# Cross-attention projections turn over three PSUM banks in a decoder layer on one NeuronCore

## The reference

```python
x = _layernorm(x + _L0_attn_ref(x, ...), axis=-1)          # causal self-attention, one head of 256
x = _layernorm(x + _L0_xattn_ref(x, ctx_2048, mask, ...), axis=-1)
x = _layernorm(x + _L0_ffn_ref(x, ...), axis=-1)           # 64 experts, 8 per token, one shared expert
...
    q = (hidden_states @ Wq + bq).reshape(b, s, NH, HD)    # 16 heads of 128
    k = (encoder_hidden_states @ Wk + bk)                  # 4 key/value heads of 128
    v = (encoder_hidden_states @ Wv + bv)
    q = _rmsnorm(q, qn_w)
    k = _rmsnorm(k, kn_w)
    scores = jnp.einsum('bhsd,bhed->bhse', q, k) * scale
    ...
    return out.transpose(0, 2, 1, 3).reshape(b, s, NH * HD) @ Wo
```

## Time and profile before

| | |
|---|---|
| median of 3 runs | 1892.0 us (1889.64 to 1893.38) |
| the profiled execution | 1891.63 us, its span 1889.9 us |
| TensorE matmul busy | 1547.4 us, 82% of the span |
| TensorE weight loads | 1255.8 us, 66% |
| VectorE busy | 1265.1 us, 67% |
| ScalarE busy | 688.6 us, 36% |
| GpSimd busy | 1050.4 us, 56% |

### The profile page before, as it was taken

The page is one execution under the profiler, slowest core; times in us unless marked ns, Lnnn a source line. Parts: engine busy times, 40 slices in busy tenths (PEclk is TensorE's granted clock), DMA queues, the critical chain, the costliest instruction groups (busy, mean ns, idle before and its releaser), DMA issues. The chain is left out here.

```text
span 1889.9 us, 34753 instructions
## 1 busy us (share of the span) xinstructions
PE 1547.4 (82%) x9744; PEld 1255.8 (66%) x9744; DVE 1265.1 (67%) x3827; ACT 688.6 (36%) x1526; POOL 1050.4 (56%) x1023
## 2 busy tenths in 40 slices
PE   4799998999899898989999864777777878787685
PEld 3687877778788787777878753555555656555453
DVE  3688877877778887888888844345555555433486
ACT  3344444343443343434344411222232222222353
POOL 3457666666566666666666742445555545555321
PEclk7799999999999999999999976889999898988799
DMA  7323231222212111121111295655565655554496
GB/s 244 118 91 104 73 106 62 94 82 89 89 62 95 63 59 67 45 75 47 66 59 52 81 277 157 182 165 160 162 182 161 181 160 172 172 167 129 169 417 278
DMA packets 182979, 246.41 MB, mean 130 GB/s; under 512 B 30972, under 2 KB 159561, under 8 KB 178388
## 3 DMA queue, kind: packets, MB, share of 16 engines
q1 hardware_dynamic: 149188, 169.71, 28.7%
q0 software_dynamic: 27648, 69.28, 10.0%
q10 hardware_dynamic: 6032, 6.13, 0.9%
HBM read 136.19 MB, written 117.19 MB: 134 GB/s over the span
## 5 line engine op out<-in xcount | busy, mean ns | idle before, releaser
L1555 POOL DMA_INDIRECT expert_out_scratch<-y,target x320 | 318.7, 996 | 296.6 <-DVE y L1779 196.0
L558 POOL DMA_INDIRECT slot_scratch<-xrow x256 | 258.7, 1010 | 188.6 <-DVE xrow L1174 117.1
L598 PE MATMUL bank_c<-wq_w,x1t 128*128 128x512 f32 x768 | 215.4, 433 | 62.9 <-DVE q_work L1016 53.7
L598 PEld LDWEIGHTS bank_c<-wq_w,x1t 128*128 128x128 f32 x768 | 154.6, 209 | 113.1 <-DVE q_work L1016 67.8
L1614 PE MATMUL bank_g<-gu,x_turned 128*128 (+1 forms) x1408 | 217.1, 303 | 14.9 <-issue 12.4
L503 POOL TENSOR_TENSOR q_rs<-q_ve,minus_half 128x8 f32<-128x8 f32 x64 | 137.4, 2147 | 146.6 <-DVE q_ve L1005 142.9
L1614 PEld LDWEIGHTS bank_g<-gu,x_turned 128*128 128x128 f32 x1408 | 194.4, 214 | 31.0 <-issue 30.5
L1633 PE MATMUL bank_y<-dp,inter_t 64*128 (+1 forms) x352 | 137.2, 473 | 85.2 <-DVE y L1779 60.0
L1671 ACT ACTIVATE x_turned<-bank_x 128x512 f32<-128x512 f32 x176 | 105.3, 598 | 272.8 <-PE bank_x L1596 161.1
L1770 DVE TENSOR_TENSOR inter<-silu,bank_g 128x128 f32<-128x128 f32 x176 | 50.2, 285 | 220.1 <-ACT silu L1678 144.7
L744 PE MATMUL bank_d<-wo_w,o2t 128*128 128x256 f32 x1536 | 194.5, 287 | 2.0 <-DVE o2t L933 2.0
(11 more groups left out here) (240 smaller groups left out, 3305.3 us busy)
## 6 DMA issues: line engine op xcount, KB each, us to landing
x_rows<-slot_scratch SPq DMA_DIRECT2D x320, 136.0 KB
results<-expert_out_scratch SPq DMA_DIRECT2D x32, 1024.0 KB, 10.1
slot_scratch<-zeros SPq DMA_DIRECT2D x16, 816.0 KB, 4.2
dp<-in_down SPq DMA_DIRECT2D x161, 64.0 KB
slot_scratch<-zeros SPq DMA_DIRECT2D x8, 1088.0 KB, 9.4
gu<-in_gate_up SPq DMA_DIRECT2D x11, 768.0 KB
expert_out_scratch<-y,target POOLq DMA_INDIRECT x320
token_row_scratch<-xrow SPq DMA_DIRECT2D x32, 136.0 KB
```

Of the source, the lines that this page charges most:

```text
L558: nc.gpsimd.indirect_dma_start(out=slot_d[:, :], out_offset=bass.IndirectOffsetOnAxis(ap=xrow[slot][:, SLOT8 + k:SLOT8 + k + 1].bitcast(U3 ...
L598: last = nc.tensor.matmul(target, left[a][:, c, :], right(b, c), start=(n == 0 and c == 0), stop=(n == len(PASSES) - 1 and c == C - 1))
L1555: nc.gpsimd.indirect_dma_start(out=y_d[:, :], out_offset=bass.IndirectOffsetOnAxis(ap=target[n % 8][:, j:j + 1], axis=0), in_=y[s % 4][:, ...
```

## The change

- Three banks take turns for the projections: `turns` is bank_c's two and bank_e. Query groups 0 to 3 use banks 0, 1, 2, 0 of it, keys bank 1, values bank 2 (bank_e).
- Query group 2 no longer waits for a bias. It waits until bank_e is free: turned keys of the previous tile copied, and the routing count of three tiles back done. Group 3 waits for bias 0, keys for bias 1 and values for bias 2.
- Since keys and values no longer pass behind biases 2 and 3 in bank_c, the query transposes wait for the fourth bias (`q_biased` 4t + 4) and `k_biased`; the wait for `v2_copied` moves to the routing transpose, which uses bank_e after the values.
- `bank_r` is another name for bank_e where the routing uses it. No instruction is added or taken away but for a few sequencer rows.

```diff
+        bank_r = bank_e[:, 0, 0:D]
+        turns = [bank_c[:, 0, :], bank_c[:, 1, :], bank_e[:, 0, :]]
...
                 if g < 2:
                     pe.wait_ge(sig["cross_masked"], 2 * t)
+                elif g == 2:
+                    pe.wait_ge(sig["kt_copied"], t)
+                    if not (isinstance(t, int) and t < 3):
+                        pe.wait_ge(sig["counted"], t - 2)
                 else:
-                    pe.wait_ge(sig["q_biased"], 4 * t + g - 1)
-                product(bank_c[:, g % 2, :], x1t, lambda b, c: wq_w[b][:, c, g * 512:(g + 1) * 512])\
+                    pe.wait_ge(sig["q_biased"], 4 * t + 1)
+                product(turns[g % 3], x1t, lambda b, c: wq_w[b][:, c, g * 512:(g + 1) * 512])\
                     .then_inc(sig["q_projected"], 1)
...
+                pe.wait_ge(sig["q_biased"], 4 * t + 2)
+                product(turns[1], ctxt, lambda b, c: wkv_w[b][:, c, 0:KW]).then_inc(sig["k_projected"], 1)
+
+            def value_project(t):
                 pe.wait_ge(sig["q_biased"], 4 * t + 3)
-                product(bank_c[:, 0, :], ctxt, lambda b, c: wkv_w[b][:, c, 0:KW]).then_inc(sig["k_projected"], 1)
-
-            def value_project(t):
-                pe.wait_ge(sig["q_biased"], 4 * t + 4)
-                product(bank_c[:, 1, :], ctxt, lambda b, c: wkv_w[b][:, c, KW:2 * KW]).then_inc(sig["v2_projected"], 1)
+                product(turns[2], ctxt, lambda b, c: wkv_w[b][:, c, KW:2 * KW]).then_inc(sig["v2_projected"], 1)
...
                 if n:
                     pe.wait_ge(sig["qt_copied"], 2 * t + 1)
                 else:
+                    pe.wait_ge(sig["q_biased"], 4 * t + 4)
                     pe.wait_ge(sig["k_biased"], t + 1)
-                    pe.wait_ge(sig["v2_copied"], t + 1)
...
                 pe.wait_ge(sig["x2_normed"], t + 1)
                 pe.wait_ge(sig["counted"], t)
-                transpose_in(bank_e[:, 0, :], xrow[slot]).then_inc(sig["x2_transposed"], 1)
+                pe.wait_ge(sig["v2_copied"], min(t + 3, TILES) if isinstance(t, int) else t + 3)
+                transpose_in(bank_r, xrow[slot]).then_inc(sig["x2_transposed"], 1)
```

More of the change, by code:

```diff
@@ L696, in key_transpose @@
                 pe.wait_ge(sig["k_normed"], t + 1)
-                if not (isinstance(t, int) and t < 2):
+                if isinstance(t, int) and t < 2:
+                    pe.wait_ge(sig["v2_copied"], t + 1)
+                else:
                     pe.wait_ge(sig["logits_copied"], t - 1)
@@ L758, in route_score @@
                 for c in range(C):
-                    last = nc.tensor.matmul(bank_e[:, 0, 0:EXPERTS + 1], x2t[:, c, :], router_w[:, c, :],
+                    last = nc.tensor.matmul(bank_r[:, 0:EXPERTS + 1], x2t[:, c, :], router_w[:, c, :],
                                             start=(c == 0), stop=(c == C - 1))
@@ L767, in rank @@
                 pe.wait_ge(sig["kt_copied"], min(t + 3, TILES) if isinstance(t, int) else t + 3)
-                nc.tensor.matmul(bank_e[:, 0, 0:EXPERTS], before[:, :], chosen[:, :], start=True, stop=True)
-                nc.tensor.matmul(bank_e[:, 0, EXPERTS:2 * EXPERTS], ones[:, :], chosen[:, :], start=True, stop=True)\
+                nc.tensor.matmul(bank_r[:, 0:EXPERTS], before[:, :], chosen[:, :], start=True, stop=True)
+                nc.tensor.matmul(bank_r[:, EXPERTS:2 * EXPERTS], ones[:, :], chosen[:, :], start=True, stop=True)\
                     .then_inc(sig["ranked"], 1)
@@ L848, in copy_values @@
                 act.wait_ge(sig["v2_biased"], t)
-                copy("v2_copied", v2_new[:, :], bank_c[:, 1, :], "v2_projected", t + 1)
+                copy("v2_copied", v2_new[:, :], turns[2], "v2_projected", t + 1)
                 if isinstance(t, int) and t == 0:
@@ L857, in copy_x2 @@
                 act.wait_ge(sig["routed"], t)
-                copy("x2t_copied", flat(x2t[:, :, :]), bank_e[:, 0, 0:D], "x2_transposed", t + 1)
+                copy("x2t_copied", flat(x2t[:, :, :]), bank_r, "x2_transposed", t + 1)
             def copy_keys(t):
@@ L998, in bias_keys @@
                 dve.wait_ge(sig["k_projected"], t + 1)
-                nc.vector.tensor_tensor(flat(k2[:, :, :]), bank_c[:, 0, :], bkv_b[:, 0:KW], ALU.add)\
+                nc.vector.tensor_tensor(flat(k2[:, :, :]), turns[1], bkv_b[:, 0:KW], ALU.add)\
                     .then_inc(sig["k_biased"], 1)
@@ L1015, in query_bias @@
                 dve.wait_ge(sig["q_projected"], 4 * t + g + 1)
-                nc.vector.tensor_tensor(q_work[:, g * 512:(g + 1) * 512], bank_c[:, g % 2, :],
+                nc.vector.tensor_tensor(q_work[:, g * 512:(g + 1) * 512], turns[g % 3],
                                         bq_b[:, g * 512:(g + 1) * 512], ALU.add).then_inc(sig["q_biased"], 1)
@@ L1087, in route_choose @@
                 dve.wait_ge(sig["routed"], n1)
-                nc.vector.tensor_copy(logits[:, :], bank_e[:, 0, 0:EXPERTS + 1]).then_inc(sig["logits_copied"], 1)
+                nc.vector.tensor_copy(logits[:, :], bank_r[:, 0:EXPERTS + 1]).then_inc(sig["logits_copied"], 1)
                 wait_alone(dve, sig["logits_copied"], n1, sig["dve_held"])
@@ L1157, in place @@
                 dve.wait_ge(sig["ranked"], n1)
-                nc.vector.tensor_tensor(ranks[:, :], bank_e[:, 0, 0:EXPERTS], count[:, :], ALU.add)\
+                nc.vector.tensor_tensor(ranks[:, :], bank_r[:, 0:EXPERTS], count[:, :], ALU.add)\
                     .then_inc(sig["placed"], 1)
-                nc.vector.tensor_tensor(count[:, :], bank_e[:, 0, EXPERTS:2 * EXPERTS], count[:, :], ALU.add)\
+                nc.vector.tensor_tensor(count[:, :], bank_r[:, EXPERTS:2 * EXPERTS], count[:, :], ALU.add)\
                     .then_inc(sig["counted"], 1)
```

## The result

The changed kernel takes 1868.1 us (median of four runs, 1857.9 to 1876.0) against 1891.3 us (four runs) for the kernel before on the same chip: ratio 0.987 (95% interval 0.983 to 0.992), some 23 us or 1.3% faster. The profiled execution took 1860.3 us, its span 1858.6; it is one of the two faster ones of the four (the others took 1875.9 and 1876.0).

A forecast was written before the change was run, and what follows sets the result against it. An attention step was taken to be as long as TensorE's free run plus VectorE's chain after the scatter burst. 1891.6 - 18.9 + 5 = 1877.7, taken as 1878 us, 0.75% faster; range 1858 to 1895, the forecast's own 1868 to 1887.

The forecast's parts named there:

- Group 2 in the third bank: Attention loop: query group 2 starts without waiting for a bias, removing VectorE's idle before biases 2 and 3: -18.9 us.
- Late-bias steps: Attention steps where biases 0 and 1 wait, 2 and 3 do not; low clock moves to transposes, keys, values: +5 us.
- rival (b): Attention loop: early-bias steps turn into the late-bias kind, which takes longer: 1908 us; chance 0.04.
- early-bias steps: Attention steps where the residual addition starts late and biases 2 and 3 wait for their groups; 1.86 us idle goes.
- Keys and values: Keys in the second bank and values in the third, each one bias earlier: no separate gain, 0.
- New waits: Routing transpose waiting for the values' copy, and extra sequencer rows: bounded by 0 and 3 us, taken as 0.
- Rival (a): Low clock falls on transposes, keys and values in every attention step, 1.2 us each: up to 1906 us; chance 0.26.
- Rival (c): The scatter burst costs less and more attention steps become like the 31.4 us one: about 1852 us; chance 0.12.
- Rival (d): Query group 2 still starts after bias 0 because the routing count comes late: 1892 us; chance within 0.16.
- What would show it: Trace signs: three query groups unbroken, idle before biases 54.7 to about 36 us, transposes' wait 21.7 to 35 or more.
- The reading of remote: VectorE's remote waits are TensorE completions coming late during GpSimd's scatter burst, visible about 1.1 us after the sixth scatter.

The follow-up runs named there:

- the filler's run: Kernel before with eight extra matmuls, results unread, into the third bank ahead of query group 2: 1884.7 us, ratio 0.998.
- group 2 only: Changed kernel with only query group 2 in the third bank, values back in a bank of bank_c: 1870.2 us, 0.988 of the kernel before.
- the two kernels of chip 10: The changed kernel unaltered once more, 1864.8 us, ratio 0.988, and group 2 only, 1870.2 us, 0.988, beside the kernel before at 1889.9 us.
- values only: Kernel before with only the values moved to the third bank, queries and keys as they were: 1887.8 us, ratio 0.998.
- the moved scatters: Changed kernel with scatters before and after GpSimd's power split none and eight, three and five, or four and four: 2042.9, 1873.3, 1834.2 us.
- four and four: Four scatters before GpSimd's power and four after, instead of six and two: changed kernel 1834.2 us, 0.952; kernel before 1836.2 us, 0.953.
- the moved burst: Changed kernel with all eight scatters sent after GpSimd's power for the residual addition's norm: 2042.9 us (one run).
- the last run: Changed kernel with scatters four and four and the key squares on ScalarE instead of GpSimd: 1612.4 us, 0.986 of the kernel before (1634.6 us).

## Why the prediction was right, and where it was wrong

The time came out inside the range and inside the forecast's own range, faster, as forecast, by 1.3% instead of 0.75%. The mechanism of the gain was right. One of the two terms had its net sign wrong, and part of the loop's gain lies in idle that the sum did not touch, so the nearness of 1878 and 1868 is in part luck. The measurement also tells less than the forecast took: its interval is 0.983 to 0.992, and not 0.2% wide to each side.

- *Group 2 in the third bank, -18.9 us.* Right: the idle before biases 2 and 3 went from 18.9 to 1.0 us, and TensorE's wait before the transposes grew by 18.8 us: VectorE's chain stayed the later one. That the two numbers agree is chance; on chip 10 this wait came to 36.3 and 33.9 us with the same gain. What the step did not ask is where those 18.9 us came from; some 8 of them were groups at the low clock (the filler's run). The sum needed no split, since the bank removes both.
- *Late-bias steps, +5 us.* This term was too large, and what the clock did as a whole went the other way. I moved the low clock from groups 2 and 3 to the transposes, keys and values, since a pause of over 2 us seemed to stay. (Six steps with a wait before bias 0 had held a low stretch before, and not four.) That does happen, but seldom and cheaply. At 826.12 a pause of 2.21 us was followed by transposes and keys at the low clock (1.97 and 2.41 us; 1.09 and 1.63 at full pace). TensorE's wait before the query transposes took up most of it (0.35 us, and 1.45 in a like step), and the step took 33.9 us instead of 33.5: 0.4 us, not 1.2. It was one step of this profile; in the second profile of the changed kernel five steps took 3.7 to 4.6 us for keys and values. In most others the pause was shorter: at 432.94 it was 1.57 us and six keys behind it took 1.64, full pace. The low level within the loop fell from 44.4 us to 10.2 (20.5 and 17.1 in the two other profiles of the changed kernel, 17.1 with group 2 only). TensorE now works through group 2 in the time it had waited, so its longest wait before a query group is 1.4 us and not 2.8. Taken at nothing, the sum would have been 1891.6 - 18.9 = 1872.7, nearer to 1868.
- *What the sum left out, -5.7 us.* The idle before the residual addition and biases 0 and 1 fell from 66.4 to 60.7. It was 61.3 and 61.1 in the two kernels of chip 10 with the same gain, but 59.1 in values only, whose time stayed, and 73.4 in the changed kernel on chip 2 against 71.4 on chip 1 before. So it varies from execution to execution and chip to chip, and I can't put it down to the change. In some steps the kind did change: rival (b) had early-bias steps become late-bias and cost; here three steps whose biases 0 and 1 had waited got a longer wait before the residual addition and none before bias 1 instead, as at 492.49 (1.07 us), and took 31.8 us against 34.2. Why is open.
- *Keys and values, 0.* Right: values only is 0.998 (0.995 to 1.001), and group 2 only has the whole gain. *New waits, 0.* Right: idle put down to issue before the query groups is 1.8 us after and was 6.1, and the values' copy hides behind the query scaling.
- *Rival (a), the low clock in every step*, did not come: pauses of 1.3 to 1.6 us went with a granted clock of 1.00 and 0.99. The warning of the Trainium skill, "TensorE: Matmul & The Clock Gate", section "A second HAM failure mode: psum-queue depth-cycling", that turning over banks with short pauses makes the clock fall back again and again, doesn't hold for this kernel; the measurement decides. *Rival (c)*, cheaper steps, came in a small way: its 1852 was not reached by any median. Its yardstick was misread, too. The step of 31.4 us was not an early-bias step without low clock as such, but one whose residual addition had waited 1.8 us; those that wait 3.2 us took 32.3 after the change, with no low clock in them. *Rival (d)* is excluded by the order of the rows.
- *What would show it.* Groups 0 to 2 without pause, no idle before biases 2 and 3, transposes' wait over 35 us, and keys and values no longer than before (2.98 to 3.03 us together before; 2.99 to 3.02 after in 27 of 28 steps, 3.78 in the one of 826.12): seen but for that step. The idle before biases came to 25.8 and not 36 in this profile, to 33 or 34 in those of chip 10. The part behind the loop moved by 3.5 us, without a cause in the change that I could find.
- *The reading of remote* as held completions was argued from one coincidence; the moved scatters now show it. But the prediction treated the burst as given. It sets how much idle there is for a bank to remove, and with four and four the bank is worth nothing measurable on the time.

## What to carry to other kernels

A further buffer is worth at most the idle that stands before its readers, so first ask what made that chain late: here sending the eight scatters four and four instead of six and two gave 4.7% with the old banks, against 1.2 to 2.0% for the third bank, and left nothing measurable of the bank's gain. When an engine's chain moves earlier by a microsecond or two, look at what it now runs beside. And time such a change on several chips: its price here hung on something that one of the chips didn't show.

## What the runs showed that I had not expected

- TensorE's results reach VectorE and ScalarE late while GpSimd sends a run of indirect DMAs: of 66.4 us of idle before the residual addition and biases 0 and 1 over 28 steps of the kernel before, 48.5 are put down to remote, up to 3.2 us at a time (4.1 on ScalarE beside the moved burst), from the fourth or fifth scatter of a run on. Three in a row left 0.8 us before the residual addition.
- One chip showed none of it with scatters as long, and runs the kernel before in 1635 us where the others take 1890 to 1925. The part behind the loop took 657 us there in the last run, and 832 to 855 in all other profiles.
- A VectorE operation on 8 columns lasts 0.17 us alone and up to 0.82 us beside a 128x512 multiply of GpSimd, with whose end it ends: 14 us over the loop.
- TensorE's granted clock fell after pauses of 2.44 and 2.75 us and of 2.21 us (826.12, after), and stayed at the upper level over ones of 1.3 to 1.6 us. It did not fall after every long one: behind a pause of 2.78 us twelve matmuls at 210.20 of the kernel before took 3.02 us, full pace, and behind one of 2.25 us at 891.68 after the change eight transposes took 1.09.
- Open: why the four runs of the changed kernel lie at about 1859 and 1876 us, what holds the completions, and why one chip is free of it.
